# Second normalisation moved into the second attention pass, and the gate and self-attention part laid out anew over seven rounds on 128 partitions

## The chip, the cores and the metric

The kernel runs on one core of one Trainium2 chip, in f32 apart from two small bf16 operands. The metric is the device time of one execution in microseconds; the median of the timed runs counts. PE is TensorE, DVE is VectorE, ACT is ScalarE, POOL is GpSimd and SP is the SyncE queue that issues the DMAs.

## The reference

The input x is 256 images x 256 channels x 7 x 7. Four blocks follow each other. Each normalises x over groups of 8 channels (32 groups an image), works on the normalised value and adds its result to x:

```
x = x + L0(gn(x))     # 1x1 convolution with the weight rows of the 256 labels, plus bias
x = x + L1(gn(x))     # linear attention: qkv 1x1, 5x5 depthwise + grouped 1x1, two sets of heads,
                      # projection, batch norm
x = x + L2(gn(x))     # gate: per group s = sum over its 8 channels, position idx of its largest s;
                      # sim = <v[idx], v> * D(distance from idx) * zero + <mean v, v> * one;
                      # gate = sigmoid((sim - mean) / (std + 1e-5) * weight + bias); v * gate
x = x + L3(gn(x))     # self-attention over 49 positions: f, g (32 rows each), hh (256), softmax, gamma
gn(v) = (v - mean_group) / sqrt(var_group + 1e-5)
```

## The kernel before

The 256 images are cut into 16 chunks of 16 images. A chunk is a tile of 128 partitions x 2 x 784 = 128x1568 (channels on partitions, two halves of 128; 16 images x 49 positions in a half). Three parts run one after the other; a part ends when all its engines have ended.

**setup_phase** gathers the weight rows of the labels and loads constants.

**layer_one_phase** walks over steps g. GA = 128 steps (8 for a chunk, each for four images) make the first pass: block 0, qkv and the attention heads that use qkv itself. 128 more make the second pass, with the aggregated (depthwise and grouped) values: a step is the pointwise matmuls `p_qkv` (L363), `p_turn` (L368), the ACT evictions `kT`, `vT`, `qr` (L613, L606, L619), `p_vk` (L378), the DVE eviction `vk` (L484), `p_out` (L390), the DVE work `den`, `rden`, `oN` (to L499), the turn back (L399) and the ACT eviction `o` (L635). These belong to consecutive groups of four images, so they lie in a staggered pipeline, and each bank is used again by the next step. The depthwise matmuls ("fills", L414) stand in fixed steps, the last of them 48 steps into the second pass; from there on the second pass holds 80 steps, ten chunks, without them. Two tables, `PE_AT` and `V_AT`, say at which of the 8 steps of a chunk and in which of three slots (a, b, c) a piece of work of another kind is done: the block-0 normalisation and matmuls, and the four projections `proj` (L437) whose DVE half is `xb<-p_g,bn_scale,xb` (L573). After the second pass's projection the chunk `xb`, which is now x after block 1, is stored to DRAM (`x2_scratch`).

**gate_and_attention_phase** does blocks 2 and 3. Each engine runs a body once a round, and a round holds six chunks of different age: `intake`, `norm2`, `gate`, `norm3`, `attend`, `leave`. The bodies are lists written by hand; an engine does them strictly in that order, and each step begins with waits on counters. A chunk is loaded twice (`x2_in` for the normalisation, `x2_gate` for the residual of block 2). On DVE one chunk needs, in 128x1568 operations: sum, centre, sum of squares and scale for norm2, `qv`, `prod` and `x3` for the gate, and sum, centre, sum of squares and scale for norm3. The gate's work per group (`v_hot`, `v_dist`, `v_sim`, `v_context`) lies on 64 partitions: 32 groups x 2 halves of the chunk, 392 columns. POOL does the power -1/2 for both norms (`g_root`, L1449), `gapped` and the standard deviation of the gate. Group sums are matmuls with the 0/1 matrix `sel` into 32 columns of the array (L1232), their inverse, from groups back to channels, matmuls with `spread` out of 32 rows of it (L1238).

## Time and profile before

| | us |
|---|---|
| median of 3 runs (2307.52 to 2308.8) | 2308.43 |
| the profiled execution | 2306.92 |
| its span | 2305.0 |
| PE busy | 1888.4 (82%) |
| DVE busy | 1408.7 (61%) |
| ACT busy | 898.2 (39%) |
| POOL busy | 274.6 (12%) |

The profiled execution took 1.9 us more than its span: the span starts with the first and ends with the last thing that the profiler records. The median of the timed runs is 1.5 us above the profiled execution. Shares of busy time are averages over stages with different limits, so the stages are read apart: the setup to 30 us, the two passes of the attention to about 1588 us, the gate and self-attention after that.

### The profile page before, as it was taken

The numbers are of one execution on the slowest core, as the hardware profiler recorded it, in microseconds if no ns is written. First come the engines' busy times: TensorE is split into PE (matmuls) and PEld (weight loads), VectorE is DVE, ScalarE is ACT, GpSimd is POOL, SyncE is SP. The second block draws the span as 40 slices with busy tenths as digits, with TensorE's granted clock in tenths as the row PEclk, the third lists the DMA queues.
The fourth block names the chain that finished last, engine by engine and source line by source line (L and its number), as shares of the span: only waits on it lengthen the run. The fifth ranks groups of instructions, "written<-read, shape, count | busy, mean of one in ns | idle before, by whom it ended". The sixth has DMA issues, their size and how long they took to land. (4 is left out here: it accounts for less than half of the span.)

```text
span 2305.0 us, 40585 instructions
## 1 busy us (share of the span) xinstructions
PE 1888.4 (82%) x15572; PEld 1215.3 (53%) x15572; DVE 1408.7 (61%) x2847; ACT 898.2 (39%) x2181; POOL 274.6 (12%) x77
## 2 busy tenths in 40 slices
PE   2799999999999999778778999994377776876768
PEld 1355555566666665566656677762134443444446
DVE  4676677765555554322222455554899989999984
ACT  0444444444444445333333444441123333233332
POOL 1000000000000000000000000001243434434340
PEclk9899999999999999899888999997578888887879
DMA  2122322375657656888878665642112112121101
GB/s 96 46 81 71 105 71 77 113 197 171 188 166 215 187 163 165 191 222 217 214 220 218 164 153 160 156 113 74 42 42 70 46 54 70 57 68 56 59 28 43
DMA packets 264469, 279.45 MB, mean 121 GB/s; under 512 B 208788, under 2 KB 234772, under 8 KB 264280
## 3 DMA queue, kind: packets, MB, share of 16 engines
q1 hardware_dynamic: 264120, 276.59, 42.8%
q8 instruction: 128, 2.10, 0.4%
q14 instruction: 61, 0.50, 0.1%
q0 software_dynamic: 160, 0.26, 0.0%
...
## 5 line engine op out<-in xcount | busy, mean ns | idle before, releaser
L484 DVE TENSOR_TENSOR vk<-p_vk,mask_vo 128x512 f32<-128x512 f32 x256 | 176.8, 691 | 556.7 <-PE p_vk L378 556.7
L1449 POOL TENSOR_TENSOR rstd<-var,minus_half 128x32 f32<-128x32 f32 x32 | 173.9, 5433 | 1896.3 <-DVE var L1025 1896.3
L414 PE MATMUL p_dw<-tw,qd 98*64 98x98 f32 x3072 | 244.0, 295 | 90.7 <-ACT agg_out L627 63.2
L414 PEld LDWEIGHTS p_dw<-tw,qd 98*64 98x64 f32 x3072 | 200.4, 206 | 154.7 <-ACT agg_out L627 80.7
L627 ACT ACTIVATE agg_out<-p_dw 128x294 f32<-128x294 f32 x256 | 106.4, 416 | 332.2 <-PE p_dw L414 254.0
L600 ACT ACTIVATE half_b<-p_qkv 98x384 f32<-98x384 f32 x256 | 125.2, 489 | 233.6 <-PE p_qkv L337 231.7
L437 PE MATMUL p_g<-o,w_proj 128*128 128x392 f32 x512 | 206.5, 529 | 3.0 <-DVE var L540 2.4
L337 PE MATMUL p_qkv<-w_qkv,half_a 128*98 128x384 f32 x512 | 190.8, 496 | 6.7 <-DVE half_a L556 6.7
L337 PE MATMUL p_qkv<-w_qkv,z_odd 128*98 128x384 f32 x512 | 190.4, 495 | 1.8 <-DVE z_odd L556 1.8
L390 PE MATMUL p_out<-vk,qr 128*49 128x136 f32 x2048 | 173.6, 291 | 1.0 <-DVE oN L499 1.0
L635 ACT ACTIVATE o<-p_turn 128x196 f32<-128x196 f32 x256 | 85.2, 333 | 163.0 <-PE p_turn L399 162.1
L1303 PE MATMUL p_b<-wv,z 128*98 128x256 f32 x512 | 146.9, 445 | 0.4 <-ACT hh L1411 0.4
L1217 PE MATMUL p_wide<-stat,mask 128*128 128x32 f32 x128 | 27.4, 317 | 119.7 <-DVE stat L1021 83.4
L399 PE MATMUL p_turn<-ident,oN 128*128 128x128 f32 x512 | 110.7, 299 | 14.9 <-ACT qr L619 14.3
L390 PEld LDWEIGHTS p_out<-vk,qr 128*49 128x49 f32 x2048 | 113.2, 128 | 16.4 <-issue 1.3
L1303 PEld LDWEIGHTS p_b<-wv,z 128*98 128x98 f32 x512 | 95.9, 196 | 48.4 <-issue 16.5
L437 PEld LDWEIGHTS p_g<-o,w_proj 128*128 128x128 f32 x512 | 91.8, 199 | 55.9 <-issue 16.3
L378 PEld LDWEIGHTS p_vk<-vT,kT 98*32 98x32 f32 x4096 | 69.9, 108 | 86.5 <-issue 82.9
L606 ACT ACTIVATE vT<-half_b,image_of 98x256 f32<-98x256 f32 x256 | 114.7, 498 | 0.0
L499 DVE TENSOR_TENSOR oN<-p_out,rden 128x256 f32<-128x256 f32 x256 | 108.7, 424 | 9.0 <-PE p_turn L399 0.2
L378 PE MATMUL p_vk<-vT,kT 98*32 98x66 f32 x4096 | 112.3, 226 | 0.0
L337 PEld LDWEIGHTS p_qkv<-w_qkv,half_a 128*98 128x98 f32 x512 | 77.9, 168 | 56.1 <-issue 45.8
...
## 6 DMA issues: line engine op xcount, KB each, us to landing
...
agg_scratch<-agg_out SPq DMA_DIRECT2D x128, 294.0 KB, 5.5
tw<-in_w_toep SPq DMA_DIRECT2D x128, 220.5 KB
...
```

The costliest lines, as they stand in the source:

```text
L337: mm = pe.matmul(p_qkv[r][0:PR, 0:QKV], z[c % 2][:, t, PR * w:PR * w + PR], W["w_qkv"][:, t, QKV * e:QKV * e + QKV], start=(t == 0), stop= ...
L378: mm = pe.matmul(p_vk[32 * c:32 * c + 32, 2 * VC * pr:2 * VC * pr + 2 * VC], kT[:, G % 2, pr, 32 * c:32 * c + 32], vT[:, G % 2, pr, :, c, ...
L390: mm = pe.matmul(out_of[64 * i:64 * i + S, pr, 0:VO], qr[:, G % 4, at:at + S], vk[:, G % 2, pr, i, :], start=True, stop=True)
L399: mm = pe.transpose(turned_of[:, pr, 0:128], oN[:, G % 2, pr, :], W["ident"][:, :])
L414: mm = pe.matmul(p_dw[NP * cp:NP * cp + NP, PR * s:PR * s + PR], qd[:, QB % 2, :, ch - QB_CH * qb], tw[:, SB % 2, :, 6 * (F % SB_FILLS) + ...
L437: mm = pe.matmul(bank[:, 0:HALF], W["w_proj"][:, q0 + e, 128 * m:128 * m + 128], o[:, n % 2, e, HALF * h:HALF * h + HALF], start=(e == 0), ...
L484: v.tensor_tensor(dst[:, :, 0:128].rearrange("p k (c n) -> p k c n", c=HC), src[:, :, 0:2 * D].unsqueeze(2).to_broadcast([128, 4, HC, 2 * D]),
L499: v.tensor_tensor(oN[:, G % 2, :, :].rearrange("p r (h d) -> p r h d", h=8), out_of[:, :, 0:128].rearrange("p r (h d) -> p r h d", h=8), r ...
L600: a.activation(raw[:, e, w, :], p_qkv[r][0:PR, 0:QKV], ACT.Copy).then_inc(raw_ev, 1)
L606: a.activation(vT[:, G % 2, :, i, :, 0:2 * D], src.rearrange("r q (c n) -> r q c n", c=HC), ACT.Copy, scale=W["image_of"][:, i:i + 1]).the ...
L1303: mm = pe.matmul(p_b[0:PR, n % 2, C * q:C * q + C], two_images(z3[it % 2][:, t, :], 2 * n + q), W["wv"][:, t, :], start=(t == 0), stop=(t ...
L1449: done(g.tensor_tensor(rstd[k][:, :, :].rearrange("p t b -> p (t b)"), var[k][:, :], W["minus_half"][:, :], ALU.pow), f"rstd{k + 2}")
```

## The change

1. The second pass of layer_one_phase does the normalisation of block 2. Six entries of the tables (`gate_sum`, `gate_centre`, `gate_square_sum`, `gate_var`, `gate_scale` on DVE, two `gate_stat` on PE) are placed two chunks behind the attention; ACT gets a square and a root for each chunk (after the steps with u == 3 and u == 6). What is stored to DRAM is the normalised `z2`, no longer x; the mean, the scaled gap and the standard deviation of every group stay in SBUF (`gate_mean`, `gate_gap`, `gate_std`). The walk over steps ends 7 steps later. The load of `xb` waits for `gate_centred`, the store for `gate_scaled`.
2. The last part loads a chunk once. Block 2's output is z2 * gate + z2 * std + mean: 1 + gate/std scales are formed on groups (`v_gate`: tanh + `one_std`), spread to channels and multiplied with z2 (`v_gated`), and the mean is added (`v_x3`).
3. The group work lies on 128 partitions (32 groups x 4 quarters of the chunk), 196 columns. The row of the largest s comes from one comparison against `row_ends` and one reduction in place of six comparisons. `sel` and `spread` matmuls are cut in quarters: `sel` ones use four column groups of 32, `spread` ones all 128 rows of the array.
4. The scale of norm3 moves from DVE (one 128x1568) to ACT (32 of 128x49, `a_scale`); the sum of the softmax is taken by ACT while it does the exponentials (`accum_out`).
5. The rounds hold seven ages in place of six (22 rounds in place of 21); z2 has 5 buffers, x3 and z3 have 3, x4 and prod 2.
6. `wv` and `wqk` are loaded at the start of the last part, no longer in the setup.

```diff
@@ -302,22 +306,30 @@
             mine = fills.get(g, [])
             return mine[slot] if slot < len(mine) else None
 
-        PE_AT = {(0, "a"): [("stat", 1, 1)], (1, "c"): [("l0", 0, 1)], (2, "a"): [("l0", 1, 1)], (2, "b"): [("l0", 2, 1)],
-                 (3, "a"): [("l0", 3, 1)], (4, "b"): [("stat", 2, 1)], (4, "c"): [("proj", 0, -1)],
+        PE_AT = {(0, "a"): [("stat", 1, 1)], (1, "c"): [("l0", 0, 1)], (2, "a"): [("gate_stat", 0, -2), ("l0", 1, 1)], (2, "b"): [("l0", 2, 1)],
+                 (3, "a"): [("l0", 3, 1)], (5, "c"): [("gate_stat", 1, -2)],
+                 (4, "b"): [("stat", 2, 1)], (4, "c"): [("proj", 0, -1)],
                  (6, "a"): [("stat", 3, 1), ("stat", 0, 2)], (6, "b"): [("proj", 1, -1)], (6, "c"): [("proj", 2, -1)],
                  (7, "b"): [("proj", 3, -1)]}
-        V_AT = {(0, "a"): [("proj", 3, -2)], (0, "b"): [("var", 0, 1)], (1, "a"): [("scale", 0, 1)],
+        V_AT = {(0, "a"): [("proj", 3, -2)], (0, "b"): [("var", 0, 1)], (0, "c"): [("gate_sum", 0, -2)],
+                (2, "c"): [("gate_centre", 0, -2)], (6, "a"): [("gate_var", 0, -2)], (1, "a"): [("scale", 0, 1)],
                 (2, "a"): [("l0", 0, 1)], (2, "b"): [("l0", 1, 1)], (3, "a"): [("l0", 2, 1)],
-                (3, "c"): [("l0", 3, 1), ("sum", 1, 1)], (4, "c"): [("centre", 1, 1)],
+                (3, "c"): [("l0", 3, 1), ("sum", 1, 1)], (4, "c"): [("gate_square_sum", 0, -2), ("centre", 1, 1)],
                 (5, "b"): [("proj", 0, -1), ("sum", 0, 2)], (5, "c"): [("square_sum", 1, 1)],
                 (6, "b"): [("var", 1, 1), ("centre", 0, 2)], (6, "c"): [("proj", 1, -1)],
-                (7, "a"): [("scale", 1, 1)], (7, "b"): [("proj", 2, -1)], (7, "c"): [("square_sum", 0, 2)]}
+                (7, "a"): [("scale", 1, 1)], (7, "b"): [("proj", 2, -1)], (7, "c"): [("gate_scale", 0, -2), ("square_sum", 0, 2)]}
...
 
+        def v_gate(v, what, n):
+
+            c2 = n - chunks
+            gate = gate_z[c2 % 2]
+            if what == "gate_sum":
+                v.wait_ge(pg_read, turn["proj", n, 3] + 1)
+                v.tensor_reduce(stat[:, 0, :], by_image(xb[:, n % 2, :, :]), AX.X, ALU.add).then_inc(gate_summed, 1)
+            elif what == "gate_centre":
+                v.wait_ge(pg_mm, turn["gate_stat", n, 0] + 1)
+                v.tensor_scalar(W["gate_mean"][:, c2, :, :].rearrange("p t b -> p (t b)"), group(("gate_stat", n, 0))[:, 0:KT * NB],
+                                1.0 / (GS * S), None, ALU.mult).then_inc(pg_read, 1)
+                v.wait_ge(pg_read, turn["gate_stat", n, 0] + 1)
+                if c2 == 0:
+                    v.wait_ge(qkv_mm, 2 * GA)
+                elif c2 == 1:
+                    v.wait_ge(pg_mm, turn["l0", chunks - 1, 3] + 1)
+                else:
+                    v.wait_ge(z2_st[c2 % 2], 16 * (c2 // 2))
+                v.tensor_tensor(by_image(gate), by_image(xb[:, n % 2, :, :]), over_positions(W["gate_mean"][:, c2, :, :]),
+                                ALU.subtract).then_inc(gate_centred, 1)
+                v.scalar_tensor_tensor(W["gate_gap"][:, c2, :, :].rearrange("p t b -> p (t b)"), stat[:, 0, :], 1.0 / S,
+                                       W["gate_mean"][:, c2, :, :].rearrange("p t b -> p (t b)"),
+                                       ALU.mult, ALU.subtract).then_inc(gap_raw, 1)
+            elif what == "gate_square_sum":
+                v.wait_ge(gate_squared, c2 + 1)
+                v.tensor_reduce(stat[:, 1, :], by_image(sq[:, :, :]), AX.X, ALU.add).then_inc(gate_summed, 1)
+            elif what == "gate_var":
+                v.wait_ge(pg_mm, turn["gate_stat", n, 1] + 1)
+                v.tensor_scalar(var[:, :], group(("gate_stat", n, 1))[:, 0:KT * NB], 1.0 / (GS * S), 1e-5,
+                                ALU.mult, ALU.add).then_inc(pg_read, 1)
+            else:
+                flat = rstd[:, :, :].rearrange("p t b -> p (t b)")
+                gap = W["gate_gap"][:, c2, :, :].rearrange("p t b -> p (t b)")
+                v.wait_ge(gate_std, c2 + 1)
+                v.reciprocal(root[:, :], std[:, :]).then_inc(gate_guess, 1)
+                v.wait_ge(gate_guess, c2 + 1)
+                v.tensor_tensor(error[:, :], root[:, :], var[:, :], ALU.mult).then_inc(gate_error, 1)
+                v.wait_ge(gate_error, 2 * c2 + 1)
+                v.scalar_tensor_tensor(error[:, :], error[:, :], -0.5, root[:, :], ALU.mult, ALU.mult).then_inc(gate_error, 1)
+                v.wait_ge(gate_error, 2 * c2 + 2)
+                v.scalar_tensor_tensor(flat, error[:, :], 1.5, root[:, :], ALU.add, ALU.mult).then_inc(gate_rstd, 1)
+                v.wait_ge(gate_rstd, c2 + 1)
+                v.wait_ge(gate_centred, c2 + 1)
+                v.tensor_tensor(by_image(gate), by_image(gate), over_positions(rstd[:, :, :]),
+                                ALU.mult).then_inc(gate_scaled, 1)
+                v.wait_ge(gap_raw, c2 + 1)
+                v.tensor_tensor(gap, gap, flat, ALU.mult).then_inc(gap_ok, 1)
+                v.tensor_tensor(W["gate_std"][:, c2, :], var[:, :], flat, ALU.mult).then_inc(gap_ok, 1)
...
+        def a_gate_square(a, c2):
+            a.wait_ge(gate_centred, c2 + 1)
+            wait(a, gate_summed, 2 * c2)
+            a.activation(sq[:, :, :], gate_z[c2 % 2], ACT.Square).then_inc(gate_squared, 1)
+
+        def a_gate_root(a, n):
+            a.wait_ge(pg_read, turn["gate_stat", n, 1] + 1)
+            wait(a, gate_guess, n - chunks)
+            a.activation(std[:, :], var[:, :], ACT.Sqrt).then_inc(gate_std, 1)
...
                 a_square(a, c + 2, 0)
+            if u == 3 and chunks <= c - 2 < NP2:
+                a_gate_square(a, c - 2 - chunks)
+            if u == 6 and chunks <= c - 2 < NP2:
...
             sp.dma_start(qt[h][:, w0:w0 + UN, QKV * e:QKV * e + QKV], raw[:, e, :, :]).then_inc(raw_st[e], 16)
 
         def sp_load_part(sp, P):
-            sp.wait_ge(xb_st[P % 2], 16 * (P // 2))
+            sp.wait_ge(xb_st[P % 2], 16 * min(P // 2, chunks // 2))
+            wait(sp, gate_centred, P - 1 - chunks)
             sp.dma_start(xb[:, P % 2, :, :], xpart[P - chunks]).then_inc(xb_in[P % 2], 16)
 
         def sp_store_part(sp, P):
             sp.wait_ge(pg_read, turn["proj", P, 3] + 1)
-            dst = xpart[P] if P < chunks else x2_out[P - chunks]
-            sp.dma_start(dst, xb[:, P % 2, :, :]).then_inc(xb_st[P % 2], 16)
+            sp.dma_start(xpart[P], xb[:, P % 2, :, :]).then_inc(xb_st[P % 2], 16)
+
+        def sp_store_gate(sp, c2):
+            sp.wait_ge(gate_scaled, c2 + 1)
+            sp.dma_start(z2_out[c2], gate_z[c2 % 2]).then_inc(z2_st[c2 % 2], 16)
...
                 sp_store_raw(sp, (g - 4) // UN, (g - 4) // 4 % 2)
-            if u == 1 and 0 <= c - 2 < NP2:
+            if u == 1 and 0 <= c - 2 < chunks:
                 sp_store_part(sp, c - 2)
-            if u == 2 and chunks <= c < NP2:
+            if u == 3 and chunks <= c < NP2:
                 sp_load_part(sp, c)
```

The two helpers of the matmuls and the lists of a round on DVE, PE and ACT:

```diff
+        def v_round(v, at):
+
+            def run(step, age, *more):
+                if at[age] is not None:
+                    step(v, at[age], *more)
+
+            run(v_x4, 6, 0)
+            run(v_x4, 6, 1)
+            run(v_ssq, 3)
+            run(v_centre, 4)
+            run(v_dsum, 2)
+            run(v_picked, 2, 1)
+            run(v_context, 3)
+            run(v_max, 5)
+            run(v_square_sum, 4)
+            run(v_qv, 2)
+            run(v_var, 4)
+            run(v_gate, 3)
+            run(v_prod, 2)
+            run(v_probs, 5)
+            run(v_gated, 3, 0)
+            run(v_find, 1)
+            run(v_hot, 1)
+            run(v_sim, 2)
+            run(v_gated, 3, 1)
+            run(v_dist, 1)
+            run(v_x3, 3)
+            run(v_sum, 3)
+            run(v_picked, 1, 0)
+
+        def pe_group_sum(pe, bank, src, name):
 
             for t in range(KT):
-                for i in range(2):
-                    mm = pe.matmul(p_group[G * i:G * i + G, 0, 0:HALF], sel[:, t, :], by_half(src[:, t, :])[:, i],
+                for q in range(4):
+                    mm = pe.matmul(bank[G * q:G * q + G, 0:QC], sel[:, t, :], src[:, t, QC * q:QC * q + QC],
                                    start=(t == 0), stop=(t == KT - 1))
             done(mm, name)
 
         def pe_spread(pe, sel_rows, src, t, name):
-            for i in range(2):
-                mm = pe.matmul(p_rows[t][:, i, 0:HALF], sel_rows[G * i:G * i + G, t, :],
-                               src[G * i:G * i + G, :], start=True, stop=True)
+
+            for q in range(4):
+                mm = pe.matmul(p_rows[:, q // 2, QC * (q % 2):QC * (q % 2) + QC], sel_rows[:, t, q, :], src[:, :],
+                               start=True, stop=True)
             done(mm, name)
 
         def pe_sums(pe, it):
-            wait(pe, "z2", it + 1)
-
-            wait(pe, "gated", 2 * it)
-            pe_group_sum(pe, z2, "s_mm")
+            z2_there(pe, it)
+
+            wait(pe, "gap_ev", it)
...
+        def pe_round(pe, at):
+            def run(step, age, *more):
+                if at[age] is not None:
+                    step(pe, at[age], *more)
+
+            run(pe_var, 5)
+            run(pe_hh, 6, 3)
+            run(pe_sums, 2)
+            run(pe_gate, 4, 0)
+            run(pe_sim, 3)
+            run(pe_turn, 6)
+            run(pe_gate, 4, 1)
+            run(pe_out, 6, 0)
+            run(pe_hot, 2, 0)
+            run(pe_gap, 2)
+            run(pe_out, 6, 1)
+            run(pe_mean, 4)
+            run(pe_fg, 5)
+            run(pe_hot, 2, 1)
+            run(pe_hh, 5, 0)
+            run(pe_scores, 5)
+            run(pe_hh, 5, 1)
+            run(pe_hh, 5, 2)
 
...
+        def a_square(a, it):
+            wait(a, "centred", it + 1)
+            wait(a, "square_sum", it)
+            done(a.activation(sq[:, :, :], zc[:, :, :], ACT.Square), "squared")
+
+        def a_scale(a, it, t):
+            wait(a, "rstd_ok", it + 1)
+
+            wait(a, "o_mm", 4 * (it + 1 - Z3S))
+            for b in range(NB):
+                i = a.activation(z3[it % Z3S][:, t, S * b:S * b + S], zc[:, t, S * b:S * b + S], ACT.Copy,
+                                 scale=rstd[:, t, b:b + 1])
+            done(i, "z3")
...
+        def a_round(a, at):
+            def run(step, age, *more):
+                if at[age] is not None:
+                    step(a, at[age], *more)
+
+            run(a_hh, 5, 2)
+            run(a_hh, 5, 3)
+            run(a_sums, 1)
+            run(a_beta, 5)
+            run(a_scale, 4, 0)
+            run(a_scale, 4, 1)
+            run(a_sim_square, 2)
+            run(a_gauss, 1)
+            run(a_fg, 4)
+            run(a_gap, 1)
+            run(a_square, 3)
+            run(a_hh, 4, 0)
+            run(a_tanh, 2)
+            run(a_hh, 4, 1)
+            run(a_exp, 4)
 
```

On DVE, in the second pass, the end of a chunk's eighth step (group of `oN`, then what slot c holds, then the projection of the next step) reads before:

```order
L573 SCALAR_TENSOR_TENSOR xb<-p_g,bn_scale,xb 128x392
L494 TENSOR_SCALAR den<-p_out 128x16
L496 RECIPROCAL rden<-den 128x16
L499 TENSOR_TENSOR oN<-p_out,rden 128x256
L573 SCALAR_TENSOR_TENSOR xb<-p_g,bn_scale,xb 128x392
L484 TENSOR_TENSOR vk<-p_vk,mask_vo 128x4x128
```

and now, with `root` to `z_odd` the step `gate_scale` and `gate_gap`, `gate_std` what it also leaves:

```order
L588 SCALAR_TENSOR_TENSOR xb<-p_g,bn_scale,xb 128x392
L509 TENSOR_SCALAR den<-p_out 128x16
L511 RECIPROCAL rden<-den 128x16
L514 TENSOR_TENSOR oN<-p_out,rden 128x256
L625 RECIPROCAL root<-std 128x32
L627 TENSOR_TENSOR error<-root,var 128x32
L629 SCALAR_TENSOR_TENSOR error<-error,root 128x32
L631 SCALAR_TENSOR_TENSOR rstd<-error,root 128x32
L634 TENSOR_TENSOR z_odd<-z_odd,rstd 128x1568
L637 TENSOR_TENSOR gate_gap<-gate_gap,rstd 128x32
L638 TENSOR_TENSOR gate_std<-var,rstd 128x32
L588 SCALAR_TENSOR_TENSOR xb<-p_g,bn_scale,xb 128x392
```

Seven instructions, one of them of 128x1568, stand between `oN` and the projection that stood next to each other.

On ACT, in the last part, the end of one round and the start of the next before (`hh` and `beta` of the self-attention, `s_sb` the group sums, `f_sb` the eviction of the block `wqk` of the next chunk):

```order
L1380 ACTIVATE simsq<-sim 64x392
L1386 ACTIVATE gate<-sim,half_par 64x392
L1411 ACTIVATE hh<-p_b 98x512
L1417 ACTIVATE beta<-p_b 98x392 x2
L1365 ACTIVATE s_sb<-p_group 64x392
L1394 ACTIVATE f_sb<-p_a 32x392
L1394 ACTIVATE g_sb<-p_a 32x392
```

and now:

```order
L1451 ACTIVATE hh<-p_b 98x512 x2
L1387 ACTIVATE s_sb<-p_sum 128x196
L1458 ACTIVATE beta<-p_b 98x392 x2
L1423 ACTIVATE z_2<-zc,rstd 128x49 x32
L1406 ACTIVATE simsq<-sim 128x196
L1398 ACTIVATE dist<-apart,rate 128x28 x2
L1401 ACTIVATE gauss<-dist,log_norm 128x56
L1433 ACTIVATE f_sb<-p_a 32x392
```

Between `beta` and the evictions of `f_sb` now stand the 32 scalings, on which the `wqk` matmuls of the same chunk wait.

On PE, in the last part, the gate's way back from groups to channels before:

```order
L1217 MATMUL p_wide<-stat,mask 128x32
L1303 MATMUL p_b<-wv,z_0 98x256 x8
L1217 MATMUL p_wide<-stat,mask 128x32
L1238 MATMUL p_wide<-gate,spread 128x392 x2
L1238 MATMUL p_group<-gate,spread 128x392 x2
```

and now, with the group sums that stand around it:

```order
L1335 MATMUL p_b<-wv,z_2 98x256 x4
L1249 MATMUL p_sum<-z_0,sel 32x196 x8
L1256 MATMUL p_rows<-gate,spread 128x196 x4
L1249 MATMUL p_stat<-prod,sel 32x196 x8
L1345 MATMUL p_b<-ident,sc 98x98 x8
L1256 MATMUL p_rows<-gate,spread 128x196 x4
```

Four matmuls of 392 columns have become eight of 196, and a group sum eight of 196 in place of four of 392.

## Rows read from the trace of the kernel before

**Rows 1.** Busy time per engine by stage; the first line names the columns.

```profile
core 0: us, PE busy (x) PEld busy (x) DVE busy (x) ACT busy (x) POOL busy (x), PEclk, DMA share, GB/s
1342.00:1550.00 208.00, 198.39 (x2320) 146.30 (x2309) 111.96 (x336) 101.36 (x305) 0.00 (x0) 1.00 0.55 145
1588.00:1723.68 135.68, 59.45 (x231) 27.38 (x232) 107.06 (x162) 27.19 (x44) 51.68 (x13) 0.62 0.16 55
1723.68:2217.29 493.61, 361.85 (x1778) 216.66 (x1778) 447.88 (x673) 157.17 (x312) 201.16 (x48) 0.83 0.18 58
2217.29:2305.00 87.71, 68.03 (x363) 46.27 (x362) 47.76 (x69) 26.66 (x61) 12.46 (x3) 0.90 0.09 37
```

**Rows 2.** Groups of DVE, last part: busy us, mean ns | idle before.

```profile
L1036 DVE TENSOR_TENSOR z<-zc,rstd 128x1568 f32<-128x1568 f32 x32 | 57.1, 1785 | 3.9 <-POOL rstd L1449 3.9
...
L995 DVE TENSOR_REDUCE stat<-x 128x32 f32<-128x1568 f32 x32 | 56.9, 1777 | 2.9 <-DMA x<-x_scratch 2.9
...
L1138 DVE SCALAR_TENSOR_TENSOR prod<-p_wide,z 128x784 f32<-128x784 f32 x16 | 15.5, 969 | 2.4 <-PE p_wide L1238 2.4
...
L1163 DVE TENSOR_REDUCE ssm<-sc 98x8 f32<-98x784 f32 x16 | 15.3, 953 | 6.3 <-ACT sc L1404 6.3
...
L1073 DVE SCALAR_TENSOR_TENSOR row<-idx,row 64x8 f32<-64x8 f32 x80 | 12.6, 158 | 2.8
...
L1056 DVE TENSOR_REDUCE best<-s_sb 64x8 f32<-64x392 f32 x16 | 8.7, 545 | 5.1 <-ACT s_sb L1365 5.1
```

**Rows 3.** Timeline of PE in one round of the last part (start us, us).

```profile
2111.12 3.67 PE L1303 MATMUL p_b<-wv,z 128*98 128x256 f32 x16
2120.41 0.64 PE L1217 MATMUL p_wide<-stat,mask 128*128 128x32 f32 x2 [5.61 <-DVE stat L1021]
...
2123.71 1.54 PE L1238 MATMUL p_group<-gate,spread 32*128 32x392 f32 x4
...
2132.67 1.51 PE L1232 MATMUL p_group<-z,sel 128*32 128x392 f32 x8
2134.11 0.93 PE L1320 MATMUL p_b<-z,ident 128*128 128x392 f32 x2
2134.87 1.03 PE L1323 MATMUL p_b<-beta,hh 98*128 98x98 f32 x8
2135.74 0.85 PE L1320 MATMUL p_b<-z,ident 128*128 128x392 f32 x2
```

**Rows 4.** Groups of POOL and ACT in the last part.

```profile
L1449 POOL TENSOR_TENSOR rstd<-var,minus_half 128x32 f32<-128x32 f32 x32 | 173.9, 5433 | 1896.3 <-DVE var L1025 1896.3
...
L1361 ACT ACTIVATE sq<-zc 128x1568 f32<-128x1568 f32 x32 | 48.3, 1510 | 93.4 <-DVE zc L1008 93.4
...
L1404 ACT ACTIVATE sc<-p_a,neg_max 98x98 f32<-98x98 f32 x128 | 31.5, 359 | 6.5 <-DVE neg_max L1159 6.5
...
L1394 ACT ACTIVATE f_sb<-p_a 32x392 f32<-32x392 f32 x32 | 15.6, 488 | 71.6 <-PE p_a L1280 71.2
```

**Rows 5.** Timeline of one step of the second pass.

```profile
1543.25 1.04 PE L363 MATMUL p_qkv<-pwbd,half_b 128*98 128x128 f32 x8
...
1544.32 0.38 ACT L613 ACTIVATE kT<-p_qkv 98x256 f32<-98x256 f32 x1 [0.54 <-PE p_qkv L363]
...
1545.06 0.69 DVE L484 TENSOR_TENSOR vk<-p_vk,mask_vo 128x512 f32<-128x512 f32 x1 [1.19 <-PE p_vk L378]
1545.32 0.34 ACT L619 ACTIVATE qr<-p_turn 128x196 f32<-128x196 f32 x1
...
1545.80 0.41 PE L399 MATMUL p_turn<-ident,oN 128*128 128x128 f32 x2 [0.21 <-ACT qr L619]
...
1546.05 1.04 PE L363 MATMUL p_qkv<-pwbd,half_b 128*98 128x128 f32 x8
1546.25 0.42 DVE L499 TENSOR_TENSOR oN<-p_out,rden 128x256 f32<-128x256 f32 x1
```

**Rows 6.** Timeline: DVE's last projection in the second pass.

```profile
1581.24 0.63 DVE L573 SCALAR_TENSOR_TENSOR xb<-p_g,bn_scale,xb 128x392 f32<-128x392 f32 x1 [0.69 <-PE p_g L437]
```

665 lines of the change are left out of this document (297 added, 368 removed).

## The prediction

> **What bounds the kernel now.** Read first the busy time by stage [rows 1]: what engine is full in which stage. In the second pass PE is busy 198 of 208 us at full clock and DVE 112. In the last part it is the other way round: between 1723.68 and 2217.29 us DVE is busy 448 of 494 us, PE 362, and PE's clock is 0.83 of full, so it spends a third of the time at 1.2 GHz and the rest at 2.4. POOL has four instructions a chunk, and 48 stand in that window: 12 rounds, 41.1 us each. The last part takes 136 + 494 + 88 = 717 us, which is 16 rounds (658 us) and 59 us for filling and draining.
>
> Then read why PE's clock falls: PE's timeline in one round [rows 3]. It waits 5.61 us for a sum of squares on DVE, and the gate's four records behind it, at 2123.71, take 1.54 us though two of them lie side by side in the array. So DVE's list sets the round, and PE comes out of its wait with a slow clock.
>
> For the second pass read one step [rows 5]. PE is nearly full, but what closes the step is a ring: `p_qkv` at 1543.25, kT at 1544.32, qr from 1545.32, then the turn L399 at 1545.80 with 0.21 us of waiting for qr, then the next `p_qkv` at 1546.05, 2.80 us after the first. ACT has 0.54 us of idle ahead of kT; DVE has 1.19 ahead of vk.
>
> **The last part, DVE.** Before, a chunk's instructions add up so [rows 2]: eleven of 128x1568 at 1.78 (19.6), six of 128x784 at 0.97 (5.8), four for the softmax 2.3 with two reductions of 0.95, twelve on 64x392 at 0.56 (6.7), some 25 small ones at 0.16 to 0.24 (about 5). Sum 39.5; the round is 41.1, so 1.6 us more than the plain sum. After:
> - norm2 (four) and the scale of norm3 leave: six of 128x1568 stay, 10.7. Six of 128x784, 5.8. Softmax without its sum, 2.4.
> - thirteen operations of 196 columns. No row has this shape; a 64x8 costs 0.158 and a 64x392 0.545 [rows 2], so 1.0 ns a column and 0.35 for 196: 4.6. Bounds: 0.16 and 0.55, that is 2 and 7. Between ends far apart I take the line through both.
> - eight small ones, 1.4.
> Sum 24.9, bounds 22 to 27.
>
> **The last part, PE, at full clock** [rows 3]: hh 32 records at 3.67/16 = 0.23, 7.3; the outputs four times 1.63 (2134.11 to 2135.74), 6.5; three group sums, 1.44 each before; scores, turn and the first projection 4.1 from the same column counts; statistics 0.6; the bf16 spread 0.7. The gate's spread was two row groups side by side, eight records of 392 columns, at full clock 8 x 0.38/2 = 1.5; over 128 rows it is 16 records one after the other of 196 columns. A 98-column record takes 0.11 (2134.87 to 2135.74 for eight), a 392-column one 0.38, so 0.20: 3.2 us. For a group sum the two column groups gave eight 392-column records in 1.44, half of 8 x 0.38. With four groups of 196 columns it is between 0.7 (four side by side) and 1.44 (still two). I take 0.7, since the records halve in length and the groups double. Sum 24.5; with 1.44, 26.7.
> The page "TensorEngine Tiling (Array Packing)" of the Trainium skill, section Tiling Modes, gives four independent tiles for 128x32 and for 32x128, and up to 4x for a small dimension. By it the sums are 0.7 us, but the same rule speaks against the gate's spread, which gives its row tiles up. No run here shows four tiles of this size.
>
> **ACT**: adds 32 scalings of 128x49. Exponentials of 98x98 end up at 31.5/128 = 0.246 us each back to back [rows 4]; that is the upper bound, half the columns take off at most half, the lower one is 0.12. I take 0.21: 6.7 us. ACT was 157/12 = 13.1 us a round, less 0.9 for the second square of 1.5 and halved small ones, is 17.8: not a bound. POOL drops one power of 5.43.
>
> **The round.** I laid one round out in the new order. PE meets the DVE results it needs (`gate_ok`, `prod`, `probs`, the gated halves) 0.5 to 2 us after they are there. Two places touch: the `wqk` matmuls wait for DVE's first `x4` half, some 0.5 us, and DVE's `v_max` waits for the scores, some 0.6. A ring goes through the round: `qv` 1.8, variance 0.2, POOL's power 5.4, 32 scalings 6.7, `wqk` 1.5, evictions 4 x 0.49, scores 1.6, `v_max` 1.1, sum of squares 1.8, handoffs about 1.2. That is 23.3, below DVE's sum. So DVE's 24.9 and the same 1.6 us of waits as before: **26.5 us a round**. PE is then 92% busy without a gap of the size of the 5.61 us, and its clock should stay up.
>
> Filling: 80 us from 1588 to PE's first full round (constants now with 512 KB of `spread`, one load, then five short rounds of about 6, 12, 20, 22 and part of 23 us, set by one chunk's chain). Twelve full rounds, 318. Draining: 24 + 23 + 20, then softmax, turn, beta, outputs, `x4` and store 20: 87. Sum 485, 61 us over 16 rounds, beside 59 before. The last part gives **717 - 485 = 232 us** back.
>
> **The second pass.** A chunk now has 8.1 us more on DVE: four of 1.70 and ten small ones. A chunk there has 304 matmul records, so 2320 of them are 7.6 chunks in 208 us, 27.3 each [rows 1]: eight steps of 2.80 and four projections at 1.2. DVE was 112/7.6 = 14.7 busy of that and comes to 22.8, 83%. It fits on average, so the question is the step. Four operations fall behind `oN`. With 1.19 us of idle ahead of vk, one of 1.7 delays vk by 0.5; vk's end (0.87 us after 1545.06) is wanted by the next `p_vk`, 2.8 us after the last, so 1.5 us of slack; `oN` ends at 1546.67 and the next `p_out` starts a little ahead of the next vk, at 1547.86, so it has about 1. The sum and the sum of squares alone cost nothing. `gate_scale` is 2.85 with its six small ones, in a step with a projection; the next step has a projection and the sum: 9.3 us of work in the two (each 1.75 for its own, 0.62 a projection) against 2.80 + 4.0 of PE time. That is 2.5 of delay less 1 of slack: 1.5, and `gate_centre` two steps on is taken up by the step between. ACT's square, 1.51 [rows 4], stands in the ring, where only 0.54 is idle: 0.9. Two statistics matmuls, 0.6. That is 3.0 us a chunk, 30 for the ten dense ones (bounds: 0.6, PE alone; 10.5, all of it), and 1 each for the four gates among the fills, where the idle of the DMA stretch covers it: **+34**. If that cover is gone, 12 instead of 4. SP now waits for `gate_scaled` ahead of the loads of the next aggregated chunk; these have most of a chunk of lead.
>
> **The tail of the pass.** The last projection ends at 1581.87 [rows 6]. Behind it come now the whole normalisation of chunk 15 with nothing beside it: sum 1.7, centre 1.9, square 1.5, sum of squares 1.7, root and its four small steps 1.3, scale 1.7, handoffs and the matmuls 2, and chunk 14's scale ahead, 2.8: **+15**. The two loads that leave the setup come back in the last part: nothing.
>
> **Sum.** Span 2305.0 - 232 + 34 + 15 = 2122; 1.9 around it, 2124; the median lies 1.5 above the profiled execution: **2125 us**.
>
> **The rivals.**
> - *The clock stays low and the engines wait for each other in the round.* If PE keeps a third of its time at 1.2 GHz, 24.5/0.83 = 29.5; the two touching waits of the layout have no room then, and the round is 30. For: PE is at 0.83 now [rows 1], and both engines have the same load. Against: the clock is 1.00 in the pass where PE is 95% busy. 2125 + 16 x 3.5 = 2181. The weaker form is the group sums at 1.44, 26.7 of PE and a round of 28: 2149.
> - *The second pass pays for each inserted operation in full.* The step's ring is closed within 0.21 us, and DVE, ACT and PE all get work. 10.5 us for ten chunks and 3 for four: 2125 - 34 + 117 = 2208. Against: 1.19 and 0.54 us of idle in every step.
> - *The second pass absorbs nearly all, and the round is 25.* 0.6 us a chunk: 2125 - 28 - 24 = 2073.
> - *Slower than before.* One mechanism: the ring through POOL and ACT. It is 16.6 us and 32 scalings. The gain of 183 us is gone when a round takes 183/16 = 11.4 more, 37.9; that needs 0.67 us for each scaling, three times what the exponentials show: 2310 and above. Little speaks for it.
> The change does what it says: the order shows four of the eleven large operations gone to the pass and one to ACT.
>
> **Chances.** Forecast (round 25.5 to 28, pass 15 to 60): 0.62. Clock or coupling: 0.17. Pass in full: 0.09. Better: 0.09. Slower: 0.02; around no change 0.01. The range from 2080 to 2195 leaves out the slower case, most of the pass in full and most of the better one, and takes in the bounds on DVE's 22 to 27 a round. A change under 0.2%, 4.6 us, could not be told from none; faster by more has 0.97.
>
> **What would show it.** DVE's intervals between two `best` reductions at 26.5 in the full rounds; DVE busy over 90% there, PE about as much with PEclk above 0.95; `p_sum` records eight in 0.35 to 0.4 us per half; the scalings at 0.21; steps of the second pass with a wait of PE for qr of about 1 us behind the square, and chunks of about 30.3 us in place of 27.3; the last store of z2 15 us later relative to the last projection. The prediction is wrong if a full round is over 28, above all by PE waiting for z3 or for `x4`, or if chunks in the second pass are longer than 34.

## The result, and the profile after

The changed kernel takes 2120.51 us (median of 4 runs, 2117.29 to 2123.34) beside 2307.97 of the kernel before (4 runs in the same session): a ratio of 0.9194, with an interval of 0.9171 to 0.9217. That is 8% less, and 4.5 us below the forecast of 2125 us. The profiled execution took 2120.16 us with a span of 2118.3, so 186.7 less than before.

Busy time by stage, the same view as [rows 1]. The stretches are nine chunks of the second pass, the filling of the last part, ten of its full rounds and the draining.

```profile
core 0: us, PE busy (x) PEld busy (x) DVE busy (x) ACT busy (x) POOL busy (x), PEclk, DMA share, GB/s
1316.00:1560.00 244.00, 222.53 (x2585) 166.24 (x2584) 189.61 (x477) 123.05 (x351) 0.00 (x0) 1.00 0.53 137
1624.00:1739.80 115.80, 73.47 (x542) 48.12 (x543) 95.04 (x150) 46.74 (x154) 33.10 (x12) 0.72 0.18 65
1739.80:2012.04 272.24, 249.54 (x1802) 183.24 (x1801) 260.77 (x372) 185.33 (x660) 92.67 (x31) 0.96 0.16 57
2012.04:2118.30 106.26, 90.86 (x556) 68.43 (x554) 61.12 (x82) 67.59 (x245) 22.62 (x7) 0.97 0.10 39
```

In the third row, which is ten rounds of 27.2 us, DVE is busy 96% and PE 92%, at a clock of 0.96 where it was 0.83. Both engines are near full, so the share of busy time no longer says which one sets the round.

Groups of DVE in those ten rounds, the view of [rows 2].

```profile
L1085 DVE TENSOR_TENSOR hot_exact<-hot,last 128x196 bf16<-128x196 f32 x10 | 28.9, 2889 | 0.3
L1159 DVE SCALAR_TENSOR_TENSOR gx<-p_rows,z 128x784 f32<-128x784 f32 x21 | 20.4, 970 | 0.0
...
L1197 DVE TENSOR_REDUCE smx<-p_a 98x8 f32<-98x784 f32 x10 | 9.7, 974 | 4.4 <-PE p_a L1323 4.4
...
L1075 DVE TENSOR_REDUCE best<-s_sb 128x4 f32<-128x196 f32 x11 | 3.8, 346 | 0.0
L1149 DVE TENSOR_TENSOR sim<-sim,sinv 128x196 f32<-128x196 f32 x10 | 3.6, 362 | 0.3
```

The operations of 196 columns take 0.35 to 0.36 us, as worked out, and DVE's only wait of note is 0.44 us a round for the scores. But the first row stands out. `hot_exact` has the same shape as L1149 and takes 2.89 us, eight times as long. Nothing in the prediction foresaw that. The timeline shows what runs beside it (start us, us):

```profile
1876.70 0.36 DVE L1079 TENSOR_REDUCE last<-hot 128x4 f32<-128x196 f32 x1
1876.95 2.81 POOL L1485 TENSOR_TENSOR gapped<-z,gate_gap 128x1568 f32<-128x1568 f32 x1
1877.01 7.34 ACT L1423 ACTIVATE z<-zc,rstd 128x49 f32<-128x49 f32 x32 [0.16 <-POOL rstd L1497]
1877.09 2.88 DVE L1085 TENSOR_TENSOR hot_exact<-hot,last 128x196 bf16<-128x196 f32 x1
...
1882.53 0.81 PE L1256 MATMUL p_rows<-hot_exact,spread_exact 128*128 128x196 bf16 x4 [1.89 <-DVE gx L1159]
```

`hot_exact` starts 0.14 us after POOL's `gapped` and ends 0.2 us after it: it stands still for as long as POOL runs. DVE comes 2.5 us later than it could to the second gated half (`gx`, L1159), and PE has waited 1.89 us for it. In the kernel before the two operations met in the other order:

```profile
2048.64 0.18 DVE L1050 TENSOR_TENSOR gapm<-gapc,rstd 128x32 f32<-128x32 f32 x1
2048.74 1.78 DVE L1036 TENSOR_TENSOR z<-zc,rstd 128x1568 f32<-128x1568 f32 x1
...
2048.90 4.30 POOL L1456 TENSOR_TENSOR gapped<-z,gapm 128x1568 f32<-128x1568 f32 x1 [3.71 <-DVE gapm L1050]
...
2050.85 0.98 DVE L1173 TENSOR_TENSOR x<-p_a,x 128x784 f32<-128x784 f32 x1 [0.33 <-PE p_a L1323]
```

There DVE's scaling was first by 0.16 us and kept its 1.78; POOL's `gapped` took 4.30 in place of 2.81. The same conflict was paid for by POOL, which had time. The last row matters later: L1173 reads one input from PSUM (`p_a`) and one from SBUF, lies wholly inside `gapped`'s remaining time, and keeps its 0.98 us, in this round and in every other full one.

One round of PE, the view of [rows 3]:

```profile
1855.30 0.81 PE L1256 MATMUL p_rows<-hot_exact,spread_exact 128*128 128x196 bf16 x4 [1.88 <-DVE gx L1159]
1856.04 1.53 PE L1249 MATMUL p_sum<-gapped,sel 128*32 128x196 f32 x16
...
1862.90 0.51 PE L1256 MATMUL p_rows<-hot_exact,spread_exact 128*128 128x196 bf16 x4
...
1872.21 0.87 PE L1249 MATMUL p_sum<-z,sel 128*32 128x196 f32 x16
1873.01 1.59 PE L1256 MATMUL p_rows<-gate,spread 128*128 128x196 f32 x8
```

A group sum of 16 records takes 0.87 us, so four lie side by side: 0.7 was forecast, 1.44 if only two did. The page "TensorEngine Tiling (Array Packing)" of the Trainium skill, section Tiling Modes, which the prediction cites, gives four tiles for 128x32, the shape of these matmuls, and the 0.87 us agree with it. The gate's spread takes 1.5 to 1.6 us for each half, 3.1 in all.

In the round shown the work behind the wait of 1.88 us is slower: 1.53 for a group sum, 0.81 for four bf16 records that take 0.51 later. The granted clock is 0.50 from 1855.2 to 1858.4 us, its lower level. The wait alone doesn't bring this about: in the round that begins at 1794.0 us the same wait of 1.89 us ends at 1801.03, the clock stays at 1.00, and the two operations take 0.50 and 0.87 us. Four of the eleven full rounds are of that kind; the seven from 1821 us on each have 3.4 us at the lower level.

Where the 186.7 us come from, between events that both traces have:

| stretch | before | after | difference | forecast |
|---|---|---|---|---|
| start to projection 0 of chunk 21 (the second pass has chunks 16 to 31; setup 1.1 shorter) | 1312.94 | 1310.46 | -2.5 | +4 |
| nine dense chunks | 245.34 | 262.17 | +16.8 | +27 |
| to projection 0 of the last chunk | 19.01 | 25.37 | +6.4 | +3 |
| from there to DVE's last operation of the pass (the end of the last projection before, `gate_std` after) | 4.58 | 21.94 | +17.4 | +15 |
| last part, from there to the end | 723.1 | 498.4 | -224.8 | -232 |

The differences add up to -186.7, the forecasts to -183. The first row is less sure than its decimals. At the end of the first pass, whose work is the same in every kernel here, the changed kernel's trace is 2.8 us ahead of the one of before, and the traces of the ten experiments are 1.1 to 7.4 us ahead.

### The profile page after: what moved, and what is told of

Its sections match the earlier page's. It is cut to its first block and busy times, and to the rows that moved or that the text cites. A ratio compares the mean times of both kernels' runs of the same rounds, so it can differ in the third digit from the quotient of the medians.

```text
span 2118.3 us, 42459 instructions
## 1 busy us (share of the span) xinstructions
PE 1828.5 (86%) x16164; PEld 1239.8 (59%) x16164; DVE 1352.2 (64%) x2754; ACT 1009.1 (48%) x2853; POOL 157.7 (7%) x61
## 5 line engine op out<-in xcount | busy, mean ns | idle before, releaser
L1485 POOL TENSOR_TENSOR gapped<-z,gate_gap 128x1568 f32<-128x1568 f32 x16 | 45.0, 2814 | 1604.4 <-DMA z<-z_scratch 1600.4
L1335 PE MATMUL p_b<-wv,z 128*98 128x256 f32 x512 | 122.9, 390 | 0.0
L1423 ACT ACTIVATE z<-zc,rstd 128x49 f32<-128x49 f32 x512 | 117.6, 321 | 10.5 <-POOL rstd L1497 10.5
L349 PEld LDWEIGHTS p_qkv<-w_qkv,z_odd 128*98 128x98 f32 x512 | 78.2, 168 | 51.1 <-issue 45.5
```

Source lines behind the costliest of these rows:

```text
L349: mm = pe.matmul(p_qkv[r][0:PR, 0:QKV], z[c % 2][:, t, PR * w:PR * w + PR], W["w_qkv"][:, t, QKV * e:QKV * e + QKV], start=(t == 0), stop= ...
L1335: mm = pe.matmul(p_b[0:PR, n % 2, C * q:C * q + C], two_images(z3[it % Z3S][:, t, :], 2 * n + q), wv[:, t, :], start=(t == 0), stop=(t == ...
L1423: i = a.activation(z3[it % Z3S][:, t, S * b:S * b + S], zc[:, t, S * b:S * b + S], ACT.Copy, scale=rstd[:, t, b:b + 1])
```

## The experiments

Each is an edit of the changed kernel. The times of before in these sessions were 2312.57 (11 runs), 2309.84 (9) and 2312.07 us (one), beside 2307.97 above. Times of different sessions, and of kernels with one run, therefore say less than the intervals between two `best` reductions, which are called rounds here.

**Does POOL's `gapped` hold DVE, and if so what of DVE?** The first edit lets `gapped` start only behind `hot_exact`.

```diff
             z2_there(g, it)
+            wait(g, "hot", it + 1)
             wait(g, "gap_mm", it)
```

> POOL's gapped waits for DVE's hot_exact of the same chunk, so that the two no longer run side by side. In the changed kernel hot_exact takes 2.88 us in the full rounds where its neighbours of the same shape take 0.36, and it ends when the 2.81 us of gapped end. Theory: it is held for as long as gapped runs; moved apart it takes 0.36, DVE's list falls from 27.3 to about 24.8, PE needs 24.4, and a round comes to 25 to 25.8: 1.5 to 2.3 us x 15 = 22 to 35 us less, some 2085 to 2098. Rival: whatever DVE operation meets gapped is held as long (the simulated gate's sim operations now, 0.4 us each otherwise), the round stays at 27.3 and the time at 2120. Second rival: DVE is not held, but gapped gets longer again, to the 4.1 us of the kernel before; then hot_exact is fast and the round 25 to 26 too.

Measured: 2126.33 us (5 runs), ratio 0.9178 (0.9155 to 0.9201), an interval that overlaps the change's own. The round is 27.34 to 27.36, but for one of 30.55. The timeline:

```profile
1880.35 0.36 DVE L1085 TENSOR_TENSOR hot_exact<-hot,last 128x196 bf16<-128x196 f32 x1
1880.63 0.41 DVE L1129 SCALAR_TENSOR_TENSOR sim<-p_stat,half_zero,dsum 128x196 f32<-128x196 f32 x1
1881.08 2.80 DVE L1132 TENSOR_TENSOR sim<-sim,gap_sim 128x196 f32<-128x196 f32 x1
1883.92 0.36 DVE L1133 TENSOR_REDUCE ssum<-sim 128x4 f32<-128x196 f32 x1
...
1880.85 2.82 POOL L1486 TENSOR_TENSOR gapped<-z,gate_gap 128x1568 f32<-128x1568 f32 x1 [0.61 <-issue]
```

`hot_exact` is back at 0.36, and the hold has moved to L1132. Between them L1129, which was under way when POOL started and reads one of its tensors from PSUM, keeps its 0.41. The first rival of the expectation came true, not its theory: it isn't a matter of `hot_exact`, but of the next DVE instruction with two inputs from SBUF. That one with an operand in PSUM is not held even when it starts in the middle of `gapped` is shown by L1173 in the trace of before.

**Is it the type?** `hot_exact` is the only one that writes bf16.

```diff
-        hot_exact = sb("hot_exact", [128, QC], mybir.dt.bfloat16)
+        hot_exact = sb("hot_exact", [128, QC])
```

(and the matrix that it is spread with, `spread_exact`, likewise.)

> hot_exact and the spread matrix of its matmuls are f32 in place of bf16. Theory: it is the two-byte output that makes DVE wait for POOL (no f32 operation beside gapped is held); then hot_exact takes about 0.4 us beside gapped, gapped takes 4 us again, DVE's list is 24.8, but PE has 16 more records of 196 columns, some 2.3 us: PE 26.7 and a round of 27 to 28, the time about 2115 to 2135. Rival: it is the kind of operation or its place beside gapped, not the type: hot_exact stays at 2.4 to 2.9.

Measured: 2139.59 us (one run), rounds of 28.2 and 29.5. The group of DVE in seven of its rounds:

```profile
L1085 DVE TENSOR_TENSOR hot_exact<-hot,last 128x196 f32<-128x196 f32 x7 | 20.2, 2889 | 0.2
```

Still 2.89 us, so the type is not the cause. The 19 us more are PE's: each half of its spread of `hot_exact` becomes eight f32 records, which take 1.59 us together where the bf16 ones took 0.51, and DVE's wait for the scores grows from 0.44 to 1.6 us a round. The rounds of 29.5 have 3.4 us at the lower clock in addition, the ones of 28.2 none.

**Is there a place where the hold costs nothing?** POOL does `gapped` of a chunk in the round before, behind the deviation, and not until DVE has written `neg_max` of the chunk three older. DVE's next two operations are then reductions with one input.

```diff
             z2_there(g, it)
+            wait(g, "neg_max", it - 3)
             wait(g, "gap_mm", it)
...
-            run(g_gapped, 1)
             run(g_deviation, 2)
+            run(g_gapped, 0)
             run(g_root, 3)
```

> POOL does gapped one age earlier, between the deviation and the power of its list, and starts it when DVE has its neg_max, so that it runs beside DVE's two large reductions (sum of squares and qv, one input each). The run with gapped behind hot_exact showed the next DVE operation with two SBUF inputs held for 2.80 us in its place. Theory: POOL's elementwise operation and a DVE operation with two SBUF inputs exclude each other, reductions and operations with a PSUM operand don't; now nothing is held, DVE's list falls by 2.4 to 24.8, PE needs 24.4: a round of 25.0 to 25.8 in place of 27.3, 20 to 33 us less, 2087 to 2100. Rival (any large operation is held by gapped, the reductions too): the reductions or gapped get 2.8 longer and the round stays at 27.3. Second rival (PE or the ring sets the round as soon as DVE is lighter): 26.5 to 27.

Measured: 2087.34 us (5 runs), ratio 0.9045 (0.9027 to 0.9063), round 24.60 (25.0 to 25.8 expected), `hot_exact` and L1132 at 0.36. The timeline of DVE and POOL:

```profile
1898.49 0.17 DVE L1200 TENSOR_SCALAR neg_max<-smx 98x8 f32<-98x8 f32 x1
1898.57 1.79 DVE L1184 TENSOR_REDUCE stat<-sq 128x32 f32<-128x1568 f32 x1
1900.27 1.78 DVE L1107 TENSOR_REDUCE qv<-pick 128x32 f32<-128x1568 f32 x1
...
1898.80 2.82 POOL L1486 TENSOR_TENSOR gapped<-z,gate_gap 128x1568 f32<-128x1568 f32 x1 [4.55 <-issue]
```

POOL needs the same 2.82 us, and both reductions keep their 1.78. Neither side pays. That is 2.6 us a round (24.71 in place of 27.31 in the mean of twelve) and 33 us in all, for a move that takes away no work. The Trainium skill has this on its page "SBUF — State Buffer", section "SBUF: two separate sides": a GpSimd operation and a DVE operation with two SBUF inputs lock a shared pair of ports for the whole instruction, and whoever is first blocks the other. By that rule `hot_exact` ends right behind `gapped`'s 1879.76, and the trace agrees with 1879.97; the kernel before shows the other order, in which DVE was first and POOL stood still.

The rule doesn't hold for each of POOL's operations, though. Its power -1/2 is a TENSOR_TENSOR that reads two SBUF tensors as well, takes 5.47 us, and holds nothing (the changed kernel again):

```profile
1871.50 5.47 POOL L1497 TENSOR_TENSOR rstd<-var,minus_half 128x32 f32<-128x32 f32 x1 [7.81 <-DVE var L1189]
1871.61 1.84 DVE L1113 TENSOR_TENSOR prod<-z,qv 128x1568 f32<-128x1568 f32 x1
...
1876.31 0.36 DVE L1078 TENSOR_TENSOR hot<-hot,countdown 128x196 f32<-128x196 f32 x1
```

L1113 starts 0.11 us behind it with two SBUF inputs and takes 1.84 us, where a lock for the whole instruction would keep it until 1876.97. Here the measurement decides: `gapped` on 128x1568 holds, the power on 128x32 doesn't. Why the two differ was not tried.

**Is DVE's list the bound of the round, or the ring through POOL and ACT?** The scaling goes back to one DVE operation of 128x1568; the 32 of ACT go.

```diff
+        def v_scale(v, it):
+            wait(v, "rstd_ok", it + 1)
+            wait(v, "o_mm", 4 * (it + 1 - Z3S))
+            done(v.tensor_tensor(by_image(z3[it % Z3S][:, :, :]), by_image(zc[:, :, :]),
+                                 over_positions(rstd[:, :, :]), ALU.mult), "z3")
...
             run(v_sim, 2)
+            run(v_scale, 4)
             run(v_gated, 3, 1)
```

> The scale of norm3 goes back to DVE as one 128x1568 operation, between v_sim and the second gated half; the 32 ACT operations go. Theory (DVE's list is the bound of a round): 1.7 us more on DVE, a round of 29.0, 15 x 1.7 = 26 us more, about 2146, less 5 us that the fill and the drain gain, since 1.8 us stand in place of 7.3 in the chain of a chunk. Rival (the ring through POOL's power and ACT's 32 scalings sets the round): a round gets shorter or stays, 2095 to 2120.

Measured: 2144.45 us (4 runs), ratio 0.9269 (0.9247 to 0.9291), rounds of 28.8 to 30.5, 29.7 in the mean. The window of nine of them:

```profile
1740.91:2007.88 266.97, 234.67 (x1622) 171.35 (x1621) 250.34 (x344) 102.64 (x306) 83.40 (x28) 0.90 0.16 55
```

The ring is 5.6 us shorter, and the round is 2.5 longer, not 1.7. So the ring doesn't bound. The 0.8 beyond DVE's own operation come with a PE clock of 0.90 in place of 0.96: PE is busy 26.1 us a round in place of 25.0 for the same work. The trace tells where they go. Three of the nine rounds have 3.4 us at the lower clock and take 28.8 to 28.9 us, which is DVE's operation and nothing more; the other six have 6.8 us of it and take 29.7 to 30.5, and in them DVE waits 1.0 to 1.7 us for PE's `p_b` (L1218), up to 0.2 in the three. So in those six rounds PE at its lower clock is part of the bound.

**The softmax's sum**, which the change gave to the exponentials' accumulator, back on DVE:

```diff
-                                      accum_out=ssm[:, h, q:q + 1]), "exp")
...
+            v_then(v, it, v.tensor_reduce(ssm[:, :, :], sc[:, :, :, :], AX.X, ALU.add), "ssm")
```

> The sum of the softmax goes back to a DVE reduction of 98x784, without accum_out. Each exponential is followed by an accumulator read on ACT, 0.32 us a pair in place of 0.24, so ACT gets 0.6 us lighter and DVE 1.0 heavier. Theory (DVE sets the round): 28.3 in place of 27.3, 12 to 16 us more, about 2135. Rival (the ring over ACT): no longer than 27.3.

Measured: 2131.88 us (one run), rounds of 28.0 to 28.3, and one of 31.48 that has 10.2 us at the lower clock (as has the one of 30.55 above). Rounds without any time at the lower clock are 28.02 here and 27.11 in the changed kernel, so 0.95 us of DVE is 0.9 us of round. This run also has a third instruction held. `gapped` starts earlier in DVE's list here, `hot_exact` is back at 0.36, and L1078, which took 0.36 beside the power above, takes 2.86 beside `gapped`:

```profile
1880.64 2.86 DVE L1078 TENSOR_TENSOR hot<-hot,countdown 128x196 f32<-128x196 f32 x1
```

**The square in the second pass**, one step later:

```diff
-    (4, "c"): [("gate_square_sum", 0, -2), ("centre", 1, 1)],
+    (4, "c"): [("centre", 1, 1)], (5, "a"): [("gate_square_sum", 0, -2)],
...
-            if u == 3 and chunks <= c - 2 < NP2:
+            if u == 4 and chunks <= c - 2 < NP2:
```

What it moves away from is this place in the changed kernel (timeline, rows of a step):

```profile
1449.23 1.50 ACT L724 ACTIVATE sq<-half_a 128x1568 f32<-128x1568 f32 x1
...
1450.63 0.38 ACT L680 ACTIVATE kT<-p_qkv 98x256 f32<-98x256 f32 x1
...
1451.61 0.35 ACT L686 ACTIVATE qr<-p_turn 128x196 f32<-128x196 f32 x1
...
1452.10 0.41 PE L411 MATMUL p_turn<-ident,oN 128*128 128x128 f32 x2 [0.96 <-ACT qr L686]
```

PE waits 0.96 us for `qr` instead of the 0.21 of every step [rows 5].

> In the second pass ACT's square of the gate norm comes one step later, after the step with u == 4, where PE does a projection and ACT idles 1.86 us ahead of kT; its sum on DVE goes to slot a of step 5, where DVE idles 1.56 us. Theory: the square is what holds the ring, PE waits 0.96 us for qr behind it where 0.21 is normal. Moved, 0.75 us a chunk go, over some ten chunks 7 to 8 us less: 2112 to 2114. Rival: the slower chunk (29.1 in place of 27.3) is DVE's backlog behind gate_scale, and nothing changes: 2119 to 2121; or the sum ahead of vk holds the next step, and it gets slower by up to 1 us a chunk: 2130.

Measured: 2115.14 us (6 runs), ratio 0.9158 (0.9131 to 0.9185), an interval that overlaps the change's own, so the times alone don't tell them apart. The traces do: a dense chunk is 28.38 us in place of 29.11, so the square cost 0.73 (0.75 expected), and the span is 5.1 us shorter.

**The scale in the second pass**, with only one of 16 images scaled (the kernel leaves the scaling of the others out):

```diff
-                v.tensor_tensor(by_image(gate), by_image(gate), over_positions(rstd[:, :, :]),
+                v.tensor_tensor(by_image(gate)[:, :, 0:1, :], by_image(gate)[:, :, 0:1, :],
```

> Leaves out 15 of 16 images in the scale of the gate norm in the second pass (DVE, 128x98 in place of 128x1568), so that z2 is not scaled. What is left of the 1.85 us by which a chunk of the second pass got longer (27.26 to 29.11; the square accounts for 0.73) is DVE's backlog behind gate_scale or PE's two statistics matmuls. Theory (forecast: 1.5 for the backlog): a chunk of about 28.3 to 28.5. Rival (statistics only, 0.6 and more): it stays above 28.9. In the tail two scales of 1.7 go, so 3 us there in either case.

Measured: 2098.53 us (one run). A dense chunk is 28.3 us, 0.8 less, and DVE's tail behind the last projection is 11.2 us in place of 12.9. The last projection starts at 1587.45 in place of 1607.01, but 4.6 us of these 19.6 are there at the end of the first pass already, which the edit doesn't touch, and 3.6 more come by projection 0 of chunk 21; so the time of this run is not the price of the scale. The rounds stay at 27.1 to 27.4.

**Both edits together**, `gapped` moved and the square later:

> Both changes, gapped beside the reductions and the square of the second pass one step later. The two lie in different parts, so their gains add up: 5 us from the square (2113.2 of span against 2118.3) and what the run with gapped alone gives; 2082 to 2095 if that is 25.

Measured: **2080.87 us** (5 runs, 2079.19 to 2082.72), ratio 0.9011 (0.8999 to 0.9023). The two gains add up, and this beats both kernels: 2% below the change. Its window over nine rounds of 24.6 us:

```profile
1752.18:1973.76 221.58, 214.09 (x1622) 161.10 (x1621) 211.36 (x335) 166.80 (x594) 83.74 (x28) 1.00 0.18 63
```

PE is now busy 97% and DVE 95%. Two more kernels ask which of them sets the round.

> This kernel has both edits of e6_reduces_and_square, and in addition the softmax's sum as a DVE reduction (0.95 us a round), as in e8_softmax_sum_on_dve. It asks what sets the round of 24.6 us there, where PE is busy 262.5 of 272.2 us and DVE 257.2. Theory, TensorE is the bound now: the round stays at 24.6 to 24.9 and the time between 2077 and 2086 us. Rival, DVE's list is still the bound: the round is 25.5 and the time is 2080.9 + 15 = 2096 us.

> This kernel has both edits of e6_reduces_and_square, and in addition hot_exact and its spread matrix are f32 in place of bf16. DVE's operation takes the same time either way, but the spread's eight records of a half go from 0.50 to 1.55 us, so TensorE gets 2.1 us a round. Theory, TensorE is the bound: the round is 26.7 us and the time 2080.9 + 33 = 2114 us. Rival, DVE's list is the bound: TensorE has 0.9 us of idle a round and takes up part of it, the round is 25.3 to 25.9 and the time 2092 to 2102 us.

Measured: 2093.86 us and a round of 25.51 with 0.95 more on DVE; 2104.81 us and a round of 25.79 with 2.1 more on PE (one run each). A window of nearly nine rounds of the kernel with more on DVE:

```profile
1751.80:1975.70 223.90, 210.90 (x1589) 156.83 (x1588) 214.28 (x337) 154.56 (x511) 80.91 (x26) 1.00 0.18 62
```

The same window of the kernel with more on PE:

```profile
1751.80:1975.70 223.90, 223.90 (x1633) 172.44 (x1632) 204.43 (x324) 161.05 (x571) 82.84 (x27) 1.00 0.19 65
```

My theory, TensorE is the bound, fell, though PE has the larger busy share. DVE's 0.95 us come back as 0.91 of round; PE's 2.1 as 1.2 (in the rival's 25.3 to 25.9, with a time 3 us above its 2102; by the end of the first pass this trace is 6 us behind the one with more on DVE, so the rounds decide and not the times), since 0.9 fit into its idle time, and only then is it busy 223.9 of 223.9 us. DVE sets the round, and PE is 0.9 us behind it.

## Why the prediction was right, step by step

**The round.** Forecast 26.5, measured 27.1 to 27.4. DVE's list was right: the mean durations of a round's 37 operations add up to 25.0 with `hot_exact` at 0.36, against 24.9. So were ACT (32 scalings in 7.34 us, 0.23 each, against 0.21) and PE (24.5 forecast; with 2.1 more it is full at 25.79, so 23.7). The step that was mis-sized is "the same 1.6 us of waits as before". The real waits are the 0.44 for the scores and up to 0.26 for `p_b`, and a DVE record begins up to 0.09 us before the one ahead of it ends (1900.27 and 1898.57 + 1.79 in the timeline above), so that 24.6 a round without the hold is even less than the plain sum. The 1.6 of before was itself such a difference: in each full round of before DVE waited 1.6 us for the sums of the mean, 0.6 for the gate's squares and 0.5 for `p_a`, 2.7 in all. In place of the 1.6 the round has 2.5 us in which `gapped` holds `hot_exact`. That the sum came out near is luck: the waits were 2.0 too high, and 2.5 us of hold were missing. The conflict could be read before the run: [rows 4] don't show `gapped`, but its 4.30 us beside DVE's scaling were in the trace, and the prediction didn't ask what made it longer than the work.

**The clock rivals.** The strong one, a third of the time at the lower clock and a round of 30, did not come: the granted clock is 0.96 and the round 27.2. The lower clock is there in seven of eleven full rounds, for 3.4 us each, and a group sum then takes 1.53 us; that is not the weaker rival's 1.44, which meant two tiles in place of four at full clock. It costs little here: the rounds without it take 27.11 or 27.12 us, those with it 27.16 to 27.36. With the hold gone the clock is 1.00.

**The last part.** 232 forecast, 224.8 measured. The twelve intervals from the fourth to the sixteenth `best` take 327.7 us against 318, so 9.7 us of the gain are missing there; filling and draining were 2.4 shorter than forecast.

**The second pass.** The mechanism held and each size was too large. A dense chunk is 1.85 us longer, not 3.0: the square 0.73 (0.9 forecast), the backlog behind `gate_scale` 0.8 (1.5), and 0.3 for the rest, to which the two statistics matmuls belong (0.6). The 0.3 supposes that the two experiments' gains add up, which no run tested. The backlog is visible as waits of PE in three places behind the scale:

```profile
1466.82 1.79 DVE L634 TENSOR_TENSOR half_a<-half_a,rstd 128x1568 f32<-128x1568 f32 x1
...
1470.20 0.44 PE L390 MATMUL p_vk<-vT,kT 98*32 98x66 f32 x16 [0.21 <-DVE vk L503]
...
1471.02 0.67 PE L402 MATMUL p_out<-vk,qr 128*49 128x136 f32 x8 [0.39 <-ACT qr L686]
...
1474.23 0.67 PE L402 MATMUL p_out<-vk,qr 128*49 128x136 f32 x8 [0.39 <-DVE oN L514]
```

They come to 1.0 us, and in the trace with the small scale all three are gone. From the end of the first pass to chunk 21, the stretch with the fills, the changed kernel takes 0.3 us more than before, and the traces of the five experiments with the same second pass between 2.7 less and 0.7 more: no sign of the 4 us, the cover was better than assumed. The first pass starts 1.1 us earlier (28.49 in place of 29.62), behind a setup with fewer loads; the prediction had "nothing", and what of the setup counts was not tried. The other 1.7 us of the 2.8 by which the first pass ends earlier are within what traces of the same code differ by.

**The ending of the pass** was sized too small, 18 with the tenth dense chunk's share against 23.7. The tail behind the last projection is the whole chain with its waits (DVE; start us, us):

```profile
1607.01 0.62 DVE L588 SCALAR_TENSOR_TENSOR xb<-p_g,bn_scale,xb 128x392 f32<-128x392 f32 x1
1607.66 1.79 DVE L597 TENSOR_REDUCE stat<-xb 128x32 f32<-128x1568 f32 x1
1610.24 0.19 DVE L600 TENSOR_SCALAR gate_mean<-p_g 128x32 f32<-128x32 f32 x1 [0.79 <-PE p_g L440]
1610.46 1.79 DVE L609 TENSOR_TENSOR half_a<-xb,gate_mean 128x1568 f32<-128x1568 f32 x1
...
1613.83 1.79 DVE L616 TENSOR_REDUCE stat<-sq 128x32 f32<-128x1568 f32 x1 [1.47 <-ACT sq L724]
...
1617.95 1.79 DVE L634 TENSOR_TENSOR half_a<-half_a,rstd 128x1568 f32<-128x1568 f32 x1
...
1619.76 0.18 DVE L638 TENSOR_TENSOR gate_std<-var,rstd 128x32 f32<-128x32 f32 x1
```

Its 12.9 us, 12.3 more than before, are about what the sum of its parts gave (11.8 without the earlier chunk's scale). What was missed lies ahead of it. The last chunk's four projections take 9.0 us from the first to the last in place of 4.0, and the period ahead of them is longer by 6.4 instead of 3.0. Chunk 14's normalisation stands between the third projection and the last, which start 3.5 us apart in place of 1.3, and PE waits in the steps ahead (0.91 us for `oN`, 1.17 for the sum of squares). PE's granted clock is 0.50 from 1589 to 1602 us, where before it was 1.00 until 1584: 12 records of the projections take 6.11 us. How much of the 5.0 and the 6.4 us the clock has, and how much the waits, was not separated.

**The sum.** Against the forecast the start came 6.5 us better, the dense chunks 10.2 better, the ending 5.8 worse and the last part 7.2 worse. They cancel to 3.7, so the fit of the total says less than the fit of its terms.

**The rivals.** "The second pass pays in full" would have shown chunks of 37.8 us; they are 29.1. The ring through POOL and ACT is closed within the round with 0.23 us a scaling, and the experiment that shortened it made the kernel slower.
